# Filling TensorE's waits in the last chain of a second attention, with five smaller edits around it

## The reference, cut to what matters

```
x = x + tanh(g_xattn[0]) * attention0(layernorm(x), ctx)      # 16 heads
x = x + tanh(g_ffn[0])   * experts0(layernorm(x))             # 8 experts, all of them, weighted
x = x + tanh(g_xattn[1]) * attention1(layernorm(x), ctx, mask) # one head of 256
x = x + tanh(g_ffn[1])   * experts1(layernorm(x))             # one expert of 8 per token, capacity 256
```

## Time and profile before

| | us |
|---|---|
| median of 3 runs (762.23 to 765.86) | 763.89 |
| the profiled execution | 764.7 |
| its span, first to last instruction | 762.9 |
| PE busy in the span | 646.4 |
| DVE busy | 521.0 |
| ACT busy | 331.2 |
| POOL busy | 229.1 |

### The profile page before, as it was taken

One profiled execution on the slowest core, in us unless ns is written; L12 is line 12 of the kernel. 1 busy time (PEld: TensorE's weight loads), 2 busy tenths in 40 slices (PEclk: granted clock), 3 DMA queues, 4 the chain that ended last, 5 costly groups with the idle time before them and its releaser, 6 DMA issues.

```text
span 762.9 us, 12648 instructions
## 1 busy us (share of the span) xinstructions
PE 646.4 (85%) x4564; PEld 546.7 (72%) x4564; DVE 521.0 (68%) x1362; ACT 331.2 (43%) x530; POOL 229.1 (30%) x155
## 2 busy tenths in 40 slices
PE   5978598899899899999799889999966931799995
PEld 4656366787678778778688777898855821799995
DVE  6877987677877866866776647479458883466662
ACT  4434155355356456456355325152523321455641
POOL 2444624566532212221014010010031242255542
PEclk9879779899999999999999999999989955799998
DMA  7303303335442242333243424434221141964700
GB/s 225 121 15 127 125 1 139 125 135 211 180 166 83 85 165 84 137 113 125 83 165 113 162 87 152 132 124 146 83 69 43 61 161 43 318 210 153 242 20 26
DMA packets 43463, 94.51 MB, mean 124 GB/s; under 512 B 3519, under 2 KB 24383, under 8 KB 42384
## 3 DMA queue, kind: packets, MB, share of 16 engines
q1 hardware_dynamic: 41344, 87.62, 33.6%
q0 software_dynamic: 2064, 6.16, 2.3%
HBM read 72.94 MB, written 21.04 MB: 123 GB/s over the span
## 4 chain that ended last, share of the span: by engine, by line
PE 65%; DVE 24%; issue 5%; ACT 2%; DMA 1%; POOL 1%; DVEq 0%; SPq 0%; ACTq 0%; POOLq 0%
PE psum L1591 43%; PE psum L2097 6%; PE psum L1668 2%; PE psum L1698 2%; PE psum L1628 2%; PE psum L1662 2%; DVE work L1063 1%; DVE scratch L266 1%; DVE x_all L1079 1%; PE psum L1635 1%; PE psum L1647 1%; DVE work L951 1%; PE psum L1962 1%; PE psum L1893 1%; PE psum L1945 1%
## 5 line engine op out<-in xcount | busy, mean ns | idle before, releaser
L1591 PE MATMUL psum<-arena 128*128 128x256 f32 (+1 forms) x2544 | 446.0, 334 | 33.8 <-DVE x_all L1079 15.6
L1591 PEld LDWEIGHTS psum<-arena 128*128 128x128 f32 x2544 | 384.5, 199 | 78.4 <-DVE x_all L1079 14.8
L2135 POOL TENSOR_TENSOR diag<-neg_ident,work 128x1024 fp32r<-128x1024 f32 x32 | 60.9, 1904 | 249.3 <-DVE work L1010 242.5
L1063 DVE TENSOR_TENSOR work<-work,psum 128x512 f32<-128x512 f32 x64 | 43.9, 686 | 62.1 <-PE psum L1591 57.3
L625 ACT ACTIVATE arena<-work 128x512 fp32r<-128x512 f32 x64 | 40.3, 630 | 90.7 <-DVE work L1063 78.7
L1079 DVE SCALAR_TENSOR_TENSOR x_all<-psum,w_exp,x_all 128x256 f32<-128x256 f32 x128 | 55.9, 479 | 27.7 <-PE psum L1591 26.9
L618 ACT ACTIVATE work<-psum 128x512 f32<-128x512 f32 x64 | 38.2, 597 | 56.8 <-PE psum L1591 56.3
L1068 DVE TENSOR_TENSOR arena<-work,arena 128x512 fp32r<-128x512 f32 x64 | 51.8, 810 | 8.7 <-ACT arena L625 8.2
L2218 POOL TENSOR_TENSOR arena<-work,arena 128x1024 fp32r<-128x1024 f32 x4 | 9.5, 2370 | 151.1 <-ACT arena L641 151.1
L1010 DVE TENSOR_REDUCE work<-psum 128x8 f32<-128x1024 f32 x32 | 39.0, 1220 | 15.7 <-PE psum L1647 15.6
L593 ACT ACTIVATE work<-psum 128x1024 f32<-128x1024 f32 x32 | 32.8, 1026 | 35.4 <-PE psum L1668 32.3
(11 more groups left out here) (194 smaller groups left out, 844.8 us busy)
## 6 DMA issues: line engine op xcount, KB each, us to landing
arena<-kept SPq DMA_DIRECT2D x24, 1024.0 KB, 5.6
work<-in_w SPq DMA_DIRECT2D x16, 1024.0 KB
kept<-arena SPq DMA_DIRECT2D x8, 1536.0 KB, 6.1
arena<-kept SPq DMA_DIRECT2D x24, 512.0 KB, 4.8
work<-in_w SPq DMA_DIRECT2D x8, 768.0 KB, 7.8
slots<-fill POOLq DMA_DIRECT2D x1, 2080.0 KB
work<-in_ctxT SPq DMA_DIRECT2D x8, 256.0 KB, 3.0
work<-in_ctxT SPq DMA_DIRECT2D x4, 512.0 KB, 5.2
```

Source lines behind the costliest of these rows:

```text
L1063: dve.tensor_tensor(gu[i % 2], gu[i % 2], ps[:, UP, :], ALU.mult).then_inc(hm, 1)
L1591: mm = pe.matmul(dst, left(i, k), right(j, k), start=(n == 0), stop=(n == 3 * K2 - 1))
L2135: pool.tensor_tensor(diag, neg_ident[:, :].rearrange("p (o q) -> p o q", o=1).to_broadcast([P, 8, P]), mx[u % 2].rearrange("p (h o) -> p h ...
```

## The change

Six edits.

1. `expert_weights` no longer divides the two best weights by their sum before it uses them. It divides once, at the end, without the bound of 1e-8; that division is folded into the multiplication by the gate. Of 11 small operations 5 are left.
2. The low part of the first expert's `w1` moves from POOL to DVE (`first_split(0, ...)`, behind `xb_low` in `turn3(None, 3)`). That of `w2` stays on DVE but now stands behind a wait for the last dispatched row (`s_disp`). ACT's high part of `w2` moves up, into `turn3(None, 3)`, before `xb_high`.
3. `keep_warm(n)`: PE issues n bf16 matmuls of 128 x 512 whose result in PSUM bank 0 nobody reads. 2 and 4 of them stand around `logits1_transpose` of groups 2 and 3. In `turn3(None, 3)` there are also 2 before `attend`, 18 after it, 5 after `xb_transpose`, and 40 after the turn. None waits for anything.
4. SP loads the slots in three pieces (tiles 0 to 1, 2 to 3, 4 to 15). The second expert's weights stand behind the second piece.
5. `slots_norm` of the next expert moves behind the fourth `hidden_low`.
6. In the very last half turn `down4` puts its second tile in bank 4 and signals each tile by itself. `rows_out` and `scatter` handle the first tile while PE makes the second; `scatter` waits for each tile apart.

```diff
             def expert_weights(g):
-                divide_by_sum(7)
                 seq(dve.tensor_tensor(r[7], r[7], over_e(rs[1]), ALU.mult))
                 seq(dve.tensor_tensor(rt[4], rt[4], rt[7], ALU.add))
-                divide_by_sum(4)
+                seq(dve.tensor_reduce(rs[2], r[4], AX.X, ALU.add))
+                seq(dve.reciprocal(rs[2], rs[2]))
...
-                dve.tensor_scalar(w_exp[g % 2], r[4], tgate[:, 2:3], None, ALU.mult).then_inc(s_wexp, 1)
+                dve.scalar_tensor_tensor(w_exp[g % 2], r[4], tgate[:, 2:3], over_e(rs[2]), ALU.mult, ALU.mult
+                                         ).then_inc(s_wexp, 1)
...
-            for n, tiles in enumerate((slice(0, 4), slice(4, B))):
+            for n, tiles in enumerate((slice(0, 2), slice(2, 4), slice(4, B))):
...
-                if n == 0:
+                if n == 1:
                     load4(1, slice(1, 2))
...
                     act.wait_ge(a1, 2 * G)
                     split(0, 0, 0)
+                    split(0, 0, 1)
...
-            split(0, 0, 1)
             slots_high(0, 0)
...
+            def first_split(a, done):
+                dve.wait_ge(w4_hi.sem, w4_hi.now(0, a + 1))
+                dve.tensor_tensor(w4[0][1][:, a, :], raw4[0][:, a, :], w4[0][0][:, a, :], ALU.subtract).then_inc(done, 1)
...
                 xb_low(gb)
-                if ga is not None:
+                if ga is None:
+                    first_split(0, w4_l1.sem)
+                else:
                     mask_and_max(ga)
...
+            dve.wait_ge(s_disp, 16 * B + 16)
+            first_split(1, w4_l2.sem)
...
-                    if more:
-                        if i == 1:
-                            dve.wait_ge(s_xs[1], 16)
-                        slots_norm(*nxt)
                     for f in range(8):
                         hidden_low(g, i, f)
+                        if more and f == 3:
+                            dve.wait_ge(s_xs[1 + i], 16)
+                            slots_norm(*nxt)
...
-            split_w2(0, 0)
...
+            def keep_warm(n):
+                for _ in range(n):
+                    pe.matmul(ps[:, 0, :], ident_b[:, :], hide[:, 0:1, :].to_broadcast([P, 4, P]), start=True, stop=True,
+                              skip_group_check=True)
             def turn3(ga, gb):
                 probs_transpose(gb)
...
+                if ga is None:
+                    keep_warm(2)
                 attend(gb)
...
+                else:
+                    keep_warm(18)
                 xb_transpose(gb)
...
+                else:
+                    keep_warm(5)
                 logits1(gb)
+                if gb >= G - 2:
+                    keep_warm(2)
                 logits1_transpose(gb)
+                if gb >= G - 2:
+                    keep_warm(4)
                 places(gb)
...
             turn3(None, 3)
+            keep_warm(40)
...
             dispatch(G - 2)
-            split_w1(0, 0)
             dispatch(G - 1)
...
-                pool.wait_ge(y4.sem, y4.now(g, i + 1))
-                pool.wait_ge(ds4.sem, ds4.now(g, i + 1))
                 pool.wait_ge(idx4.sem, idx4.now(g, i + 1))
                 alone(pool)
-                for j in range(2):
+                for j, rows in enumerate((ds4, y4)):
+                    pool.wait_ge(rows.sem, rows.now(g, i + 1))
+                    alone(pool)
                     pool.indirect_dma_start(...)
```

More of the change, by code:

```diff
@@ L335, in block_kernel @@
         oh1, loc1, dest = sem("onehot_ready"), sem("places_ready"), sem("rows_ready")
-        s_xs = [sem("first_slots_loaded"), sem("other_slots_loaded")]
+        s_xs = [sem(f"{n}_slots_loaded") for n in ("first", "second", "other")]
         s_raw4 = [sem(f"expert1_weights_loaded{i}") for i in range(2)]
@@ L348, in block_kernel @@
         s_sc = [sem(f"rows_scattered{i}") for i in range(2)]
+        d4_first = sem("last_out_first_tile_ready")
         ds4 = Steps(sem("vector_step4"), 2)
@@ L1100, in first_of_max @@
                 seq(dve.tensor_tensor(dst, dst, over_e(rs[3]), ALU.is_equal))
[L1102 to L1106, removed]
             def routing_z(g):
@@ L1546, in hidden_low, with rows_out @@
                                          ).then_inc(h1_lo.sem, 1)
-            def rows_out(g, i):
-                dve.wait_ge(d4.sem, d4.now(g, i + 1))
+            def rows_out(g, i, last):
+                if last:
+                    dve.wait_ge(d4_first, 1)
+                else:
+                    dve.wait_ge(d4.sem, d4.now(g, i + 1))
                 dve.wait_ge(out_left.sem, out_left.before(g, i + 1))
@@ L1554, in rows_out @@
                 for j in range(2):
+                    if last and j:
+                        dve.wait_ge(d4.sem, d4.now(g, i + 1))
                     row = xs[:, t + j, :] if isinstance(g, int) else xs[:, bass.ds(t + j, 1), :].rearrange("p a c -> p (a c)")
-                    ins = dve.scalar_tensor_tensor(yo[i][j], ps[:, 4 + i, j * D:(j + 1) * D], row[:, D + 2:D + 3],
+                    ins = dve.scalar_tensor_tensor(yo[i][j], ps[:, 4 if last and j else 4 + i, j * D:(j + 1) * D], row[:, D + 2:D + 3],
                                                    row[:, 0:D], ALU.mult, ALU.add)
@@ L1572, in turn @@
                         split_w2(*nxt)
-                    rows_out(g, i)
-            split_w2(0, 0)
+                    rows_out(g, i, last and i == 1)
             dve.wait_ge(s_xs[0], 16)
@@ L2086, in hidden, with down4 @@
                         lambda b, k: diT[i][b][:, k, :]).then_inc(h1.sem, 1)
-            def down4(g, i):
+            def down4(g, i, last):
                 pe.wait_ge(w4_hi.sem, w4_hi.now(g, 2 * i + 2))
@@ L2091, in down4 @@
                 pe.wait_ge(y4.sem, y4.before(g, i + 1))
+                if last:
+                    pe.wait_ge(y4.sem, y4.now(g, 1))
                 for j in range(2):
+                    bank = 4 if last and j else 4 + i
                     for f in range(8):
@@ L2096, in down4 @@
                         for n, (a, b) in enumerate(THREE):
-                            mm = pe.matmul(ps[:, 4 + i, j * D:(j + 1) * D], h4[i][a][:, f, j * P:(j + 1) * P],
+                            mm = pe.matmul(ps[:, bank, j * D:(j + 1) * D], h4[i][a][:, f, j * P:(j + 1) * P],
                                            w4[i][b][:, 1, f * D:(f + 1) * D], start=(f == 0 and n == 0), stop=(f == 7 and n == 2))
+                    if last and j == 0:
+                        mm.then_inc(d4_first, 1)
                 mm.then_inc(d4.sem, 1)
@@ L2106, in turn @@
                         slots_transposed(*((g, 1) if i == 0 else (g + 1, 0)))
-                    down4(g, i)
+                    down4(g, i, last and i == 1)
             slots_transposed(0, 0)
```

## The result

The changed kernel takes 779.24 us (median of four, 775.67 to 782.23) where the kernel before takes 763.06 (median of four, 758.21 to 765.86): a ratio of 1.0217, 95% interval 1.0146 to 1.0288. It is slower, by about 2%. I had forecast 748, faster.

What follows compares the result with a forecast made beforehand. TensorE was taken to bound most of the kernel, except the four routings, attention1's last turn and the end. Terms summed to 16.5 us off a profiled 764.7, giving 748.2, left at 748; range 744 to 753.

Steps and rivals of the forecast that it cites:

- my own term for edit 2: Last turn of attention1: a root operation of VectorE ends with POOL's subtraction; without POOL's work there 4.2 us go.
- the one I gave for "slower": Added products: each occupies the queue 0.42 us at full clock, twice that at half; time about 780, chance 0.04.
- Routing, 5.2: Four routings: six of eleven dependent VectorE operations go, 1.3 us each time, 5.2 us in all; bounds 0 and 7.
- POOL's split, 4.2: Root of attention1's last turn: moving w1's first low part off POOL frees a caught VectorE operation, 4.2 us.
- the dispatch, 1.1: POOL's second indirect transfer: no longer under VectorE's other split, 0.97 instead of 2.11 us; gain 1.1, bounds 0 and 1.2.
- The added products, 1.5 + 1.5: Last turn of attention1: a held clock saves 1.5 us in attend and 1.5 from the logits to pick_expert.
- The slots in pieces, 0.8: First slots' load: 260 KB instead of 520 KB, formerly 3.75 us; gain 0.8, bounds 0 and 1.9, limited to 1.4.
- a bound of -1 only: First hidden, after the 40 products: lower bound, the second expert's weights coming later behind ScalarE's split.
- The 40, 0.4 for an earlier rise: First hidden, after the last turn: clock expected at 0.50; 0.4 us for an earlier rise, bounds -1 and +2.9.
- The end, 1.8: After TensorE's last product: one transfer issue instead of two, ending 755.4 instead of 757.17; gain 1.8, bounds 1.2 and 2.4.

Runs made afterwards that it cites:

- norm_back: The changed kernel with slots_norm put back ahead of the eight hidden_low, all else kept: 743.2 us, ratio 0.973.
- gpsimd_split_back: norm_back with the first low part of w1 on GpSimd again, between its last two dispatches, without first_split(0, ...): 751.14 us, ratio 0.9832.
- before_norm_late: The kernel before with only slots_norm moved, behind the fourth hidden_low: 800.35 us, ratio 1.0477.

## Why the prediction was wrong

The step that failed is edit 5: "0, bounds -0.5 and +0.5", because VectorE's work was "within a half turn that TensorE fills". It cost 34 us by the half turns, 36 and 37 by two pairs of medians. TensorE filled the half turn only as long as its transposes found the normalised tiles. I asked whether VectorE had the time, and not what runs beside it in the new place. The sentence at the start that the engines meet only at semaphores has the same hole: no semaphore stands between `slots_norm` and POOL's split, and yet the one waits for the other. Yet the same collision was in my own term for edit 2: a 128x4 operation that takes 4.38 us under POOL's 4.49. The timeline of a half turn before shows a split of 4.66 us by POOL that starts 4.8 us into the half turn, and the fourth eviction ends there. I never put the two together. The Trainium skill (SBUF — State Buffer, "Who interferes with whom") has a rule for it: VectorE and GpSimd share a pair of ports, a tensor_scalar can take it when its operands meet certain conditions, so can an operation with two inputs in SBUF while GpSimd reads SBUF, and whoever comes second waits for the whole instruction. The length of the wait agrees: 4.3 us for an operation of 0.4 or 0.28 beside a split of 4.6, and 0.41 where the split is cut short. That the cause is a port no run shows; the runs show that POOL's operation is. This was a rival that I did not name, and the one I gave for "slower" (products that occupy 0.42 us each) was not it; the 18 took 4.05 us and the 40 took 8.79.

The other terms, by the traces:
- Routing, 5.2: TensorE's wait before the gated add is 1.2 us in the last group instead of 2.83; all ten such waits lose 5.7, and alone the edit measured 6.7.
- POOL's split, 4.2, and the dispatch, 1.1: L266, the one that was caught, takes 0.16 us in the last turn, and the longest operation of that root is 0.29 us (L263), where I had said that none would be over 0.2; the four indirect transfers 0.97 each, and from the first of them to SP's load 6.4 us instead of 7.6.
- The added products, 1.5 + 1.5: 1.99 for 3.78 and 1.63 for 2.90. The level held through the 2.3 us wait. Worth 2.7 together.
- The slots in pieces, 0.8: back 2.9 us after the last row instead of 3.75. But now the second expert's weights come late for ScalarE: TensorE waits 1.1 us for it in norm_back and 2.7 in the changed kernel, where the kernel before has no such wait. I had this in a bound of -1 only.
- The 40, 0.4 for an earlier rise: not had. From the slots' first transposes to the first `down4` it is 12.0 us in norm_back and 11.8 before.
- The end, 1.8: in norm_back the second indirect transfer starts 1.4 us after TensorE's last product, before it was 3.2.

The terms sum to 16.5 us, and norm_back is 19.8 us faster than the kernel before beside it. Of the 3.3 us more, the routing has 1.5; the rest was not taken apart and is no more than the medians move. The other 1.7 us between my 748.2 and the 743.2 are the start: I subtracted from one execution of 764.7, and the median beside norm_back is 763.0. From `attend` to the slots my terms said 9.1 us and the trace says 9.4.

## What to carry to other kernels

An operation of VectorE from SBUF to SBUF can have a cost that depends on what GpSimd does at that moment (0.4 or 4.3 us here): before moving one, even by a few places in its own queue, lay GpSimd's long operations beside its old and its new place. A blocked operation that is short, and so looks free, can cost what is left of the other. A held clock is only worth what the next wait leaves of it: look for the transfer that the faster stretch will meet.

## What the runs showed of the hardware

- Which operation is caught depends on the moment: L266 before, L263 in gpsimd_split_back, `slots_norm` after. Each ended within 0.2 us of the end of POOL's operation, whatever its type and size: 128x4 int32 with constants 4.90 us, 128x256 with columns 4.27, with constants 4.26. Who comes first is not settled by the trace: L263's record starts 0.35 us ahead of POOL's, but POOL's spans are rough.
- VectorE's evictions, with one input in PSUM and one in SBUF, ran beside POOL's split at 0.42 us each, in both kernels.
- While a tensor_tensor of VectorE with both inputs in SBUF ran, an indirect transfer's issue on POOL took 2.11 us; once it no longer lay there, none of the four was over 0.99. In before_norm_late, where it lies there again, it is 2.12.
- Sixteen more bf16 products of 128x512 made a row of 40 longer by 3.46 us at full clock (8.79 to 12.25): 0.216 us each. In these traces the level after a wait of 2.3 us behind such a row was 1.00; after waits of 3.2 us (experts1), 3.75 us (behind the 40) and 6.9 us it was 0.50.
